# A fused decoder layer: what the second attention needs at its start is prepared inside the first

## The reference

```python
def _L0_attn_ref(x, Wqkv, bqkv, Wln, bln):
    qkv = x @ Wqkv + bqkv
    q, k, v = jnp.split(qkv, 3, axis=2)
    q = q - q.mean(axis=2, keepdims=True)
    k = k - k.mean(axis=2, keepdims=True)
    q2 = q * q
    k2 = k * k
    q2 = q2 / (q2.sum(axis=2, keepdims=True) + EPS_SUM)
    q2 = _l2norm(q2, axis=-1)
    k2 = k2 / (k2.sum(axis=2, keepdims=True) + EPS_SUM)
    k2 = _l2norm(k2, axis=-2)
    kv = jnp.einsum('bnc,bnd->bcd', k2, v)
    t2 = jnp.einsum('bnc,bcd->bnd', q2, kv) / math.sqrt(N)
    return (v + t2) @ Wln + bln
...
x = x + _L0_attn_ref(_layernorm(x), ...)             # first attention
x = x + _L0_xattn_ref(_layernorm(x), ctx, ctx, ...)  # second: 16 heads of 64, causal softmax
x = x + _L0_ffn_ref(_layernorm(x), ...)              # 16 experts, the best 4 of each token
```

## Time and profile before

| | us |
|---|---|
| median of three runs | 1788.26 (1785.36 to 1789.88) |
| the profiled execution | 1789.64, its span 1787.6 |
| PE busy | 1614.6 (90%) |
| DVE busy | 1141.9 (64%) |
| ACT busy | 1062.0 (59%) |
| POOL busy | 504.3 (28%) |

### The profile page before, as it was taken

The page is one execution under the profiler, slowest core; times in us unless marked ns, Lnnn a source line. Parts: engine busy times, 40 slices in busy tenths (PEclk is TensorE's granted clock), DMA queues, the critical chain, the costliest instruction groups (busy, mean ns, idle before and its releaser), DMA issues. The chain is left out here.

```text
span 1787.6 us, 35077 instructions
## 1 busy us (share of the span) xinstructions
PE 1614.6 (90%) x12210; PEld 1348.9 (75%) x12210; DVE 1141.9 (64%) x2600; ACT 1062.0 (59%) x2712; POOL 504.3 (28%) x433
## 2 busy tenths in 40 slices
PE   5999859999999999999999999973599999999995
PEld 4888746777676776776777777752599999999995
DVE  6999647657667577577575775633456666666662
ACT  4555337757757577477575674640366666666563
POOL 2444210000300302103003012033156545554544
PEclk9999879999999999999999999986799999999998
DMA  2122021111210221212112101077577877777873
GB/s 84 42 70 71 37 57 60 37 59 36 95 52 29 98 72 49 97 36 92 49 37 98 54 20 44 1 297 270 167 151 175 183 174 178 172 177 160 176 175 49
DMA packets 106381, 178.06 MB, mean 100 GB/s; under 512 B 13744, under 2 KB 52192, under 8 KB 106208
## 3 DMA queue, kind: packets, MB, share of 16 engines
q1 hardware_dynamic: 71808, 134.75, 23.4%
q0 software_dynamic: 28896, 38.62, 11.7%
q10 hardware_dynamic: 5504, 2.45, 0.6%
HBM read 107.53 MB, written 68.24 MB: 98 GB/s over the span
## 5 line engine op out<-in xcount | busy, mean ns | idle before, releaser
L1128 ACT ACTIVATE xa_prob<-xa_S,xa_nmax 128x512 f32<-128x512 f32 (+3 forms) x512 | 266.0, 534 | 141.8 <-DVE xa_nmax L1252 133.1
L1688 POOL DMA_INDIRECT out<-ex_y,ex_x x158 | 259.1, 1640 | 262.9 <-ACT ex_y L1637 138.9
L1591 PE MATMUL ex_H<-ex_xT,ex_w 128*128 128x256 f32 x1896 | 250.1, 289 | 7.9 <-DVE ex_xT L1657 7.9
L1591 PEld LDWEIGHTS ex_H<-ex_xT,ex_w 128*128 128x128 f32 x1896 | 236.0, 194 | 8.3 <-issue 8.3
L1605 PE MATMUL ex_Y<-experts_w_hi,ex_hT 128*128 x1264 | 234.2, 279 | 0.0
L1252 DVE TENSOR_REDUCE xa_nmax<-xa_S 128x2 f32<-128x1024 f32 (+3 forms) x256 | 198.1, 815 | 28.3 <-PE xa_S L989 20.1
L1491 POOL DMA_INDIRECT expert_rows<-xa_xn,xa_rows x128 | 125.0, 976 | 274.0 <-DVE xa_prob L1264 226.4
L1605 PEld LDWEIGHTS ex_Y<-experts_w_hi,ex_hT 128*128 128x128 f32 x1264 | 199.0, 188 | 0.0
L1663 DVE TENSOR_TENSOR ex_hT<-ex_h,ex_hT 128x512 fp32r<-128x512 f32 x158 | 109.5, 694 | 126.9 <-ACT ex_hT L1630 100.1
L1142 ACT ACTIVATE xa_probT<-xa_work 128x512 f32<-128x512 f32 x256 | 139.7, 604 | 71.5 <-PE xa_work L1001 71.0
L1605 PE MATMUL ex_Y<-experts_w_lo,ex_hT 128*128 x632 | 176.8, 280 | 0.0
(11 more groups left out here) (282 smaller groups left out, 3349.7 us busy)
## 6 DMA issues: line engine op xcount, KB each, us to landing
ex_w_raw<-in_w SPq DMA_DIRECT2D x79, 512.0 KB
ex_x<-expert_rows SPq DMA_DIRECT2D x79, 273.0 KB
w_split<-xa_w_split SPq DMA_DIRECT2D x32, 512.0 KB, 2.7
xa_w_split<-in_w SPq DMA_DIRECT2D x32, 256.0 KB
experts_w_hi<-w_split SPq DMA_DIRECT2D x16, 512.0 KB
experts_w_lo<-w_split SPq DMA_DIRECT2D x16, 512.0 KB, 10.3
expert_rows<-xa_x SPq DMA_DIRECT2D x16, 273.0 KB
a_x<-in_x SPq DMA_DIRECT2D x8, 512.0 KB, 4.1
```

What stands on the lines that cost most here:

```text
L1128: m = act.activation(prob[n % 2][:, odd, PROB_AT[i]:PROB_AT[i] + width], SB[slot[at]][:, odd, col:col + width], ACT.Exp, bias=nmax[n % 2][ ...
L1591: m = pe.matmul(bank[:, (f % 2) * ROWS:(f % 2 + 1) * ROWS], ww[:, c, f * P:(f + 1) * P], xx[:, c, :], start=(i == 0), stop=(i == len(terms ...
L1688: pool.indirect_dma_start(out, bass.IndirectOffsetOnAxis(x_in[j % NX][:, a, ID:ID + 1].bitcast(I32), 0), y[j % NY][:, a, :], None, compute ...
```

## The change

- A class `Ahead` owns what both attentions use: identity, masks, small weights and biases, tables, the buffer of the context (`ctx32`), of x1 of batch 0 (`x1_0`), of normalised x (`xn`), and the split transposed x and context of batch 0 (`xT0`, `cT0`). The first attention uses `xT0` and `ctx32` itself (ctx32 for weights and chunks).
- The first attention's POOL makes the constants before its loop, its SyncE loads the small tensors after x(1). Its DVE prepares b2 in iteration 1, half masks and bq in iteration 2. Iteration 7 takes the context of batch 0 in the way of a chunk; `find_mean(8)`, `normalise(8)` and `transpose_x(8)` treat x1 of batch 0, which is loaded back in iteration 4; POOL adds bo in iteration 8.
- The second attention's list starts with k, v tile 0, q, v tile 1; v tiles 2 and 3 stand behind the first scores. SyncE's final wait for the stores is gone from the first attention; the second one waits for them where it loads x1 or reuses it.
- knorm: `max` reads PSUM, POOL's power of -0.5 gives the inverse; two DVE steps are left out.
- x has three buffers; xb is written over x; x(b + 2) is loaded after `take_y` of b - 1.
- Beginning: an ACTIVATE on a small tile early on ScalarE, `normalise(0)` before the weights' split, the combined weight after the first two qk tiles, `find_mean(1)` and `normalise(1)` before vv of batch 0.
- Some tiles share space: stage with x1, WvT with kvT, bvB with kvl.

```diff
@@ first_attention, sync
+            w.wait_ge(b2_zero, 0)
+            for i, at in enumerate(GATE_AT):
+                sp.dma_start(b2[at:at + E], d['b2']).then_inc(b2_in.of(i), 16)
+            for name, tile in (("bq", ahead.bqT), ("bk", ahead.bkT), ("bv", ahead.bvT)):
+                sp.dma_start(tile[:], d[name].rearrange("(k p) -> p k", p=P), allow_slow_non_contiguous=True
+                             ).then_inc(small_in.of(name + "T"), 16)
...
+                if b == len(chunks) + 1:
+                    w.wait_ge(chunk_lo, len(chunks) - 1)
+                    sp.dma_start(ahead.ctx32[:], rows_of_ctx(0)).then_inc(ctx_in.of(0), 16)
+                if b == 4:
+                    w.wait_ge(x1_stored[0], 0)
+                    sp.dma_start(ahead.x1_0[:], x1_dram[0]).then_inc(x1_back.of(0), 16)
+                if b >= 1:
+                    w.wait_ge(work_ev, ("y", b - 1, 1))
                 if b + 2 < B:
-                    w.wait_ge(x_norm, b)
-                    w.wait_ge(xb_ev, (b, 1))
                     load(b + 2)
...
-            w.wait_ge(x1_stored[0], B - 2)
-            w.wait_ge(x1_stored[1], B - 1)
@@ first_attention, tensor, project(b, u)
+                    if kind == "vv" and (b, u) == (0, 0):
+                        combine_weights()
@@ first_attention, scalar
+            w.wait_ge(ones_set, "power")
+            act.activation(warm[:], power[:], ACT.Identity)
@@ first_attention, vector
+            find_mean(1)
             for b in range(B + 1):
...
+                    if b == 0:
+                        normalise(1)
+                        w.wait_ge(vl_hi, "weight")
+                        dve.tensor_tensor(Wall[1][:, :, 768:1024], KV[:].rearrange("p (k n) -> p k n", k=KC),
...
+                if b == 1:
+                    get_b2_ready()
+                if b == 2:
+                    repeat_halves()
...
-                    dve.tensor_copy(knorm[:], NB[:, 0:4].rearrange("p (c j) -> p c j", j=2)[:, :, 0]).then_inc(kn_copy.of(done), 1)
+                    dve.tensor_scalar(knorm[:], NB[:, 0:4].rearrange("p (c j) -> p c j", j=2)[:, :, 0], EPS_NORM ** 2, None, ALU.max
+                                      ).then_inc(kn_max.of(done), 1)
                 if b < B:
                     take_qk(b, 2)
-                if done >= 0:
-                    w.wait_ge(kn_root, done)
-                    dve.tensor_scalar(knorm[:], knorm[:], EPS_NORM, None, ALU.max).then_inc(kn_max.of(done), 1)
-                    w.wait_ge(kn_max, done)
-                    dve.reciprocal(knorm[:], knorm[:]).then_inc(kn_inv.of(done), 1)
-                if b < B:
                     take_qk(b, 3)
@@ first_attention, gpsimd
-                    pool.tensor_tensor(knorm[:], knorm[:], half[:, 0:KC], op=ALU.pow).then_inc(kn_root.of(done), 1)
+                    pool.tensor_tensor(knorm[:], knorm[:], power[:, 0:KC], op=ALU.pow).then_inc(kn_inv.of(done), 1)
@@ attention_plan
-    plan = [("load", 0), ("split_ctx", 0), ("lower_ctx", 0), ("find2", 0), ("norm2", 0), ("project_k", 0)]
-    plan += [("project_v", (0, t)) for t in range(N_TILES)]
-    plan += [("transpose_x", (0, 0)), ("transpose_x", (0, 1)), ("project_q", 0)]
+    plan = [("project_k", 0), ("project_v", (0, 0)), ("project_q", 0), ("project_v", (0, 1))]
...
+        start = [("project_v", (0, t)) for t in (2, 3)] if n == 0 else []
+        plan += [("scores", (n, 3)), ("scores", (n, 2)), *start, *turns[0:2], ("soften", (n, 3)), *turns[2:4], ("soften", (n, 2))]
@@ cross_attention, scalar
-            act.dma_start(bqT[:], d['bq'].rearrange("(k p) -> p k", p=P), allow_slow_non_contiguous=True
-                          ).then_inc(bias_in.of("bqT"), 16)
...
-            w.wait_ge(const_p, "b2")
-            for i, at in enumerate(GATE_AT):
-                act.dma_start(b2[at:at + E], d['b2']).then_inc(b2_in.of(i), 16)
```

399 lines of the change are left out of this document (202 added, 197 removed).

## The result

The changed kernel takes 1769.78 us (median of four runs, 1759.7 to 1772.09) where the kernel before took 1788.27 in the same session (four runs, 1785.36 to 1789.88): a ratio of 0.989, 95% interval 0.9855 to 0.9925. A second set of five runs in another session gave 0.9889 (0.9875 to 0.9903). The forecast was 1771 with a range of 1762 to 1780.

What follows compares the result with a forecast made beforehand. PE and DVE were taken as nearly full in the first attention's loop, DVE's order setting its 23.25 us period, with TensorE idle 18 us at the seam. Terms summed to -17.3 from 1789.64: 1772.3, or 1771 in runs, range 1762 to 1780.

Steps and rivals of the forecast that it cites:

- Seam, -21.8: Between the two attentions: last `take_y` to the scores of pair 1 shortens by 21.8 us, ends 18.5 and 22.6.
- 0.8 for the clock: At the second attention's first projections: 0.8 us allowed for PE's clock, between 0 (full speed) and 4.1 (half speed).
- The meeting: After the last `take_y`: SyncE issues its store (0.33) without waiting and the engines meet some 0.4 us later.
- rival (4): At the seam: first matmul still some 14 us after the engines meet, sum -3.4, time 1785; chance 0.02.
- The v tiles' price: Second attention's head: two v tiles ahead of softening cost 2.8 us of what could be won.
- knorm, -3.8: First attention's loop: two DVE steps leave, saving 0.63 us in each of six chunk iterations; ends 0 and -5.6.
- x loads, +5.0: Iterations 2 to 6: x lands late, DVE waits and its rstd step falls under POOL's add, 1.0 us each.
- b2 +2.3: Iteration 1: b2's three DVE steps come under POOL's add and cost 2.3 us; ends 1.0 and 2.5.
- masks +1.2: Iteration 2: eight half copies and bq's scaling, during POOL's power, cost 1.2 us; ends 1.0 and 3.3.
- Iteration 7, +1.4: First attention's iteration 7 becomes like the chunk iterations and costs 1.4 us more; ends 0 and 2.1.
- Start, -1.6: Kernel's start: PE projects near 16.4, wall_lo about 25.3, xT_lo of x(1) ends 1.6 us earlier; ends -4 and +1.
- announced signs: Marks expected in the trace: periods near 23.6, x waits 0.5 to 1.5, iteration 7 near 22.5, PE's first projection before 17.

Runs made afterwards that it cites:

- after_again: The changed kernel itself, unchanged, run again in another session: ratio 0.9889 to the kernel before.
- x_four: The changed kernel with a fourth x buffer, so that x(3) to x(6) load an iteration or more ahead: ratio 0.9889 to the kernel before.
- chunk_first: The changed kernel with weight chunks and context loaded as soon as POOL is done with the one before: ratio 0.9901 to the kernel before.
- start_pool: The changed kernel with POOL's memsets and iotas for the second attention moved to the first attention's last pass: ratio 0.9898 to the kernel before.
- b2_late: The changed kernel with b2's preparation, the half copies and bq's scaling moved to the first attention's last pass: ratio 0.9856 to the kernel before.
- end_wait: The changed kernel with SyncE's wait for the last two x1 stores put back at the first attention's end: ratio 0.9921 to the kernel before.
- v_late: The changed kernel with v tiles 2 and 3 of the first pair taken behind project_q of pair 1: ratio 0.9889 to the kernel before.
- knorm_alone: The kernel before with only the short knorm chain (max from PSUM, POOL's power giving the inverse): ratio 0.9961 to the kernel before.
- best: The changed kernel with weigh_q's steps moved ahead and the edits of x_four, b2_late, chunk_first, start_pool and v_late together: 1742.77 us, ratio 0.9838 to the kernel before.

## Why the prediction was right, step by step

The time and the sign were right, and the largest step was right to within 1 us. Of the small terms knorm was worth more than forecast, x, b2 and masks cost less, and iteration 7 cost more. What the sum left out are the spells of half clock in the loop.

- **Seam, -21.8.** Measured -22.5 at full clock, -20.9 with the spell of half clock that after_again, x_four, chunk_first and start_pool show in the same head (18.5 or 18.6; b2_late has 17.0). The forecast's 0.8 for the clock was the middle of what happened. The meeting, 0.76, the three projections and both scores came where they were put; rival (4) is out, first matmul 0.8 after the last `take_y`. Of these 22 us the end wait is 2.3 (end_wait). The v tiles' price was put at 2.8; it is 1.8 (v_late).
- **knorm, -3.8.** The step mis-sized. That PE's own chain before y would then come last cut it from 0.94 to 0.63 an iteration. But PE had waited 1.1 to 1.8 there before and still waits 0.3 to 0.9 in knorm_alone, so nothing had to be taken off: alone the short chain brings 5.6, the upper end that was given, and undone in the changed kernel it costs 7.8 at equal half clock. The stall moved to `weigh_q` as told, but to its first step: I took a multiply with two SBUF inputs to be free of POOL's split, and it was held 2.04.
- **x loads, +5.0.** The wait (0.2 to 0.7) and the rstd step under POOL's add are both there, 1.14 together (1.44 - 0.30) in four of five iterations of the first profile. That makes 4.6 us there and 2.5 to 3.7 in the three others, so 5.0 was high. Taking them away gained nothing that shows (x_four): in iterations 3 and 4 the chunk, which DVE waits for next, held it instead, and against after_again, the profile with as much half clock, only the 1.1 of iteration 2 was there to be gained, since x_four keeps the wait of iteration 6.
- **b2 +2.3 and masks +1.2.** The steps took 2.0 and 1.3 (73.77 to 75.09), near what was worked out. Without them (b2_late) iteration 7 ends 2.0 earlier, not 3.5: iteration 1 took up more than half of its part. The eight copies ran in 0.18 to 0.19 each under POOL's power (73.94 to 75.02), as the row foretold. The Trainium skill, "SBUF — State Buffer", section "SBUF: two separate sides", also counts a VectorE operation with two SBUF inputs among those that a GpSimd operation reading SBUF locks out; the trace agrees with that part (2.04, 2.06), which I had overlooked, and for the power it again does not.
- **Iteration 7, +1.4.** Measured +2.2 to +2.4, just over its upper end of 2.1: a full iteration beside 21.1. The prediction's own 23.25 - 0.6 - 21.1 is 1.55, not 1.4.
- **Start, -1.6.** PE's first projection at 16.21 (16.4 forecast), wall_lo at 24.14 (25.3), and still only a little came of it: iteration 1 ends 0.8 to 2.4 earlier over the four profiles with b2 in it.
- **Clock in the loop, not in the sum.** The prediction weighed half clock for the head and the start only. In the loop PE now waits up to 2.6 before the y products (1.1 to 1.8 before the change, in iterations 1 to 6). In all profiles the spells of half clock between 45 us and the end of iteration 7, thirteen in eight kernels, follow such a wait, of 1.9 to 3.7; not every such wait is followed by one (after_again, with 2.61 in iteration 2, has none). One more spell puts the end of iteration 7 1.1 to 1.6 later.
- **Sum.** Without knorm the first attention's edits were to cost 8.3 by the end of iteration 7 and cost 9.8 (7.1 to 11.1), 8.2 at equal half clock; with knorm 4.5 and 4.2 (1.5 to 5.5), 2.6 at equal half clock. The time came out near 1771 because these errors are small beside the seam and partly cancel. Of the announced signs, periods near 23.6 came at 22.4 to 25.8 in single iterations, outside the 22.8 to 25 that were to hold, and at 23.8 to 24.3 in the mean of iterations 2 to 6. The wait for x was 0.19 to 0.71, and none in iteration 4, instead of 0.5 to 1.5 throughout. Iteration 7 took 23.4 instead of 22.5, and the long step was the multiply ahead of the scalar one. Those of the seam and PE's start showed.

## What to carry to other kernels

Work that doesn't depend on the stage before it is best done inside that stage: 22 of 39 us went at a seam where three engines had waited for loads and splits, at a price of 8 to 10 us in the loop that took it in; choosing better places for the steps, `weigh_q` among them, brought 9.7 to 12.5 back (best against after_again and the changed kernel). When a stall of one engine under another's long instruction is taken away by deleting the held instruction, look at which one stands next in the queue; here only moving every SBUF-to-SBUF step out of that stretch ended it. And where two engines are nearly full, an edit's worth depends on the others: the short chain brought 5.6 alone and some 8 beside them, and chunks loaded early brought under 1 alone and 2.2 in the combination. Last, before two end times are compared, the granted clock up to there has to be compared: four profiles of the same code differed by 4 us in the order of their half clock.
